# Attention rounds in another order: the last values' low half ahead of choosing experts, positions and places later, one-hots and slot matmuls in the next round

## The reference, cut to what matters

```
x = layernorm(x + attention(x))                 # 16 heads, biases on q, k, v, out
x = layernorm(x + cross(ctx, ctx, x, mask))     # 1 head of 64
probs = softmax(x @ gate.T); topw, topi = top_k(probs, 8); topw /= topw.sum(-1)
oh = one_hot(topi); pos = (cumsum(oh) * oh).sum(-1) - 1     # a token's slot in its expert
x = layernorm(x + sum over the 8 of topw * expert(x))       # slots 512 and up are dropped
```

## Time and profile before

| what | us |
|---|---|
| median of 3 runs | 2437.91 |
| the three runs | 2436.63, 2457.16, 2437.91 |
| span of the profiled execution | 2440.0 |
| attention rounds in it | to about 1440 |

### The profile page before, as it was taken

One profiled execution on the slowest core, in us unless ns is written; L12 is line 12 of the kernel. 1 busy time (PEld: TensorE's weight loads), 2 busy tenths in 40 slices (PEclk: granted clock), 3 DMA queues, 4 the chain that ended last, 5 costly groups with the idle time before them and its releaser, 6 DMA issues.

```text
span 2440.0 us, 43737 instructions
## 1 busy us (share of the span) xinstructions
PE 2110.9 (87%) x15590; PEld 1281.1 (53%) x15590; DVE 1495.3 (61%) x2527; ACT 1198.8 (49%) x2878; POOL 1150.7 (47%) x865
## 2 busy tenths in 40 slices
PE   7898998998899899889989669888888888888891
PEld 5565666666566666656666334444444444444440
DVE  5567678768767876876787764444444444444443
ACT  6675565666556655655655313333333333333334
POOL 2454455455445544544554314444444544454542
PEclk9999999999999999999999779999999999999995
DMA  5211110110111011001101127665555656665648
GB/s 187 79 40 32 36 41 22 47 34 27 33 34 39 21 47 34 31 29 34 39 21 39 53 61 216 149 146 146 146 146 146 147 146 147 151 152 145 152 70 292
DMA packets 110249, 217.13 MB, mean 89 GB/s; under 512 B 10224, under 2 KB 32752, under 8 KB 110192
## 3 DMA queue, kind: packets, MB, share of 16 engines
q1 hardware_dynamic: 81248, 148.20, 17.7%
q0 software_dynamic: 28944, 68.17, 15.2%
HBM read 156.58 MB, written 59.77 MB: 89 GB/s over the span
## 4 chain that ended last, share of the span: by engine, by line
PE 43%; issue 15%; DMA 14%; POOL 12%; DVE 10%; ACT 5%; POOLq 1%; DVEq 0%; SPq 0%; ACTq 0%
PE bank L476 23%; DMA arena_p<-x_rows,cur_from 8%; PE bank L812 7%; DMA acc_rows<-arena_wo,cur_to 6%; POOL arena_p L1706 3%; PE bank L542 3%; PE bank L554 3%; POOL arena_p L1615 3%; POOL acc_rows L1712 3%; PE bank L799 2%; DVE s_max L1147 2%; DVE x L1194 2%; ACT arena_p L887 1%; PE bank L514 1%; POOL qk L1610 1%
## 5 line engine op out<-in xcount | busy, mean ns | idle before, releaser
L476 PE MATMUL bank<-arena_v,arena_wo 128*128 128x512 f16 x2304 | 502.7, 379 | 1.1 <-issue 1.1
L1615 POOL TENSOR_TENSOR arena_p<-arena_p,s_rden 128x1024 f32<-128x1024 f32 x128 | 272.6, 2130 | 430.7 <-DVE s_rden L1155 430.7
L1712 POOL DMA_INDIRECT acc_rows<-arena_wo,cur_to x128 | 202.3, 1581 | 446.4 <-ACT arena_wo L1086 400.2
L476 PE MATMUL bank<-xt,arena_wo 128*128 128x256 f16 x3072 | 379.9, 283 | 4.2 <-DVE arena_wo L1116 4.0
L476 PEld LDWEIGHTS bank<-arena_v,arena_wo 128*128 128x128 f16 x2304 | 225.4, 98 | 272.9 <-issue 1.6
L476 PEld LDWEIGHTS bank<-xt,arena_wo 128*128 128x128 f16 x3072 | 301.6, 102 | 75.6 <-issue 29.2
L887 ACT ACTIVATE arena_p<-bank,s_neg 128x256 f32<-128x256 f32 x512 | 235.5, 474 | 170.6 <-DVE s_neg L1150 170.6
L1116 DVE SCALAR_TENSOR_TENSOR arena_v<-bank,arena_v 128x512 f16<-128x512 f32 x192 | 130.4, 688 | 281.8 <-ACT arena_v L1064 213.7
L1116 DVE SCALAR_TENSOR_TENSOR arena_wo<-stage,arena_wo 128x3072 f16<-128x3072 f32 (+2 forms) x74 | 182.0, 2461 | 184.0 <-ACT arena_wo L959 163.2
L812 PE MATMUL bank<-arena_wo 128*128 128x512 f16 x1152 | 294.0, 410 | 0.7 <-DVE arena_wo L1552 0.7
L1706 POOL DMA_INDIRECT arena_p<-x_rows,cur_from x128 | 228.0, 1782 | 56.0 <-issue 29.3
(11 more groups left out here) (170 smaller groups left out, 3318.4 us busy)
## 6 DMA issues: line engine op xcount, KB each, us to landing
stage<-wguT SPq DMA_DIRECT2D x32, 1536.0 KB, 8.1
stage<-wdnT SPq DMA_DIRECT2D x32, 768.0 KB, 9.5
xt<-xT SPq DMA_DIRECT2D x16, 512.0 KB, 5.1
xr<-x_rows SPq DMA_DIRECT2D x16, 512.0 KB, 3.9
stage<-ctxT SPq DMA_DIRECT2D x16, 512.0 KB, 3.7
x_rows<-x SPq DMA_DIRECT2D x16, 512.0 KB, 2.9
acc_rows<-x SPq DMA_DIRECT2D x16, 512.0 KB, 4.1
arena_wo<-acc_rows SPq DMA_DIRECT2D x8, 1024.0 KB, 10.8
```

What stands on the lines that cost most here:

```text
L476: mm = pe.matmul(out_ap, lhs(a, i), rhs(c, i), start=(n == 0 and i == 0), stop=(n == 2 and i == chunks - 1))
L1615: gp.tensor_tensor(rows, rows, s_rden[:, j % 2, :].unsqueeze(2).to_broadcast([P, 4, S]), ALU.mult)\
L1712: gp.indirect_dma_start(acc_rows, bass.IndirectOffsetOnAxis(ap=cur_to[:, k, c:c + 1], axis=0), y[:, k, c, :], None, compute_op=ALU.add).th ...
```

## The change

Parts of each round stand at other places; no computation is added or left out.
- DVE: `values_lo(b, 3)` comes ahead of `choose`; `choose` stands between the two `x1_lo` of step 6 and loses its last five operations to a new function `share`. `places` goes from step 6 to step 7. `share` and `tell` go to the start of the next round, behind `masked`. The one-hots of the first half go from step 7 and behind it to steps 0 and 1 of the next round, those of the second half from steps 0 and 1 to steps 3 and 4 of that round, with their `add_slots` behind them.
- PE: `positions` goes to step 7, `fill_slots(f, 0)` from step 0 to step 2, `fill_slots(f, 1)` from step 2 to step 4. In step 1 `cross_turn` and `cross_weigh` go behind q and k of pair 1, with `values(b, 1)` between them.
- ACT: `exp2` goes behind the exponentials of pair 6; `turned2_hi` goes to the end of step 1, ahead of `values_hi(b, 1)`, and `o2_high` behind that.
- POOL: `normalise2` goes behind the scaling of pair 6.
- The counts of the semaphore `rt` follow the new order. `cross_q` now waits until `places` has read the positions (`POS_READ`), in place of `turn_x1(t, 1)`; `positions` waits for both `x1_lo`.
- The last three rounds (16 to 18) get the same, apart from the exceptions for `last` and `late_fill`.

```diff
@@ values (PE)
-                if g == 0 and fill:
-                    pe.wait_ge(slot_done, count(b - 3, 2, 1))
-                elif g == 0 and tail:
+                if g == 0 and tail:
                     past(pe, kv_lo, count(b - 1, 2))
                 if g:
                     pe.wait_ge(v_lo, count(b, 4, g))
-                if g == 2 and fill:
-                    pe.wait_ge(slot_done, count(b - 3, 2, 2))
+                if g >= 2 and fill:
+                    pe.wait_ge(slot_done, count(b - 3, 2, g - 1))
@@ turn_x1, cross_q, positions (PE)
                 elif t and route:
-                    pe.wait_ge(rt, count(b - 1, RT, 20))
+                    pe.wait_ge(rt_exp, count(b - 1, 1, 1))
...
-            def cross_q(b, last=False):
+            def cross_q(b, route):
                 pe.wait_ge(x1t_lo, count(b, TT, TT))
-                if last:
-                    pe.wait_ge(rt, count(b - 1, RT, 20))
+                if route:
+                    pe.wait_ge(rt, count(b - 1, RT, POS_READ))
...
                 pe.wait_ge(rt, count(b, RT, 11))
+                if tail:
+                    pe.wait_ge(x1t_lo, count(b + 1, TT, TT))
@@ work (PE)
-                step(0, [(fill and not late_fill, lambda: fill_slots(f, 0, head))])
+                step(0)
                 if head:
                     values(b, 0, tail, fill)
-                step(1, [(route, lambda: cross_turn(u))])
+                step(1)
+                if route:
+                    cross_turn(u)
+                if head:
+                    values(b, 1, tail, fill)
                 if route:
                     cross_weigh(u)
-                if head:
-                    values(b, 1, tail, fill)
-                step(2, [(late_fill, lambda: fill_slots(f, 0, head)), (route, lambda: cross_project(u, 0)),
-                         (fill and not last and not late_fill, lambda: fill_slots(f, 1, head))])
+                step(2, [(route, lambda: cross_project(u, 0)), (fill, lambda: fill_slots(f, 0, head))])
...
-                step(4, [(tail, lambda: project(t, 0, route))])
+                step(4, [(tail, lambda: project(t, 0, route)), (fill and not late_fill, lambda: fill_slots(f, 1, head))])
...
-                step(6, [(tail, lambda: turn_x1(t, 0, head, route, fill)), (route, lambda: positions(u))])
+                step(6, [(tail, lambda: turn_x1(t, 0, head, route, fill)), (late_fill, lambda: positions(u, tail))])
...
-                step(7, [(tail, lambda: ctx_kv(t)), (tail, lambda: cross_q(t))])
+                step(7, [(route and not late_fill, lambda: positions(u, tail)), (tail, lambda: ctx_kv(t)),
+                         (tail, lambda: cross_q(t, route))])
@@ work (ACT)
-                step(0, first=[(route, lambda: exp2(u))])
+                step(0, between=[(route, lambda: exp2(u))])
...
-                step(1, first=[(route, lambda: turned2_hi(u))])
+                step(1)
+                if route:
+                    turned2_hi(u)
+                if head:
+                    values_hi(b, 1)
                 if route:
                     o2_high(u)
-                if head:
-                    values_hi(b, 1)
@@ work (DVE)
+                if fill and not late_fill and not (isinstance(r, int) and r == B + 2):
+                    share(f)
+                    tell(f)
...
-                step(0, [(route, lambda: row_scales2(u))], soon=[(fill and not late_fill, lambda: add_slots(f, 0))])
-                if late_fill:
-                    slot_onehot(f, 0, 0)
-                elif fill and not last:
-                    slot_onehot(f, 1, 0)
+                step(0)
+                if route:
+                    row_scales2(u)
                 if head:
                     values_lo(b, 0)
+                if fill:
+                    slot_onehot(f, 0, 0)
...
-                step(1, [(route, lambda: turned2_lo(u)), (fill and not last, lambda: slot_onehot(f, 0 if late_fill else 1, 1))])
+                step(1, [(fill, lambda: slot_onehot(f, 0, 1))])
+                if route:
+                    turned2_lo(u)
+                if head:
+                    values_lo(b, 1)
                 if route:
                     o2_low(u)
-                if late_fill:
-                    slot_onehot(f, 1, 0)
-                if head:
-                    values_lo(b, 1)
...
-                if fill and not last:
-                    add_slots(f, 0 if late_fill else 1)
+                if fill:
+                    add_slots(f, 0)
...
+                if fill:
+                    slot_onehot(f, 1, 0)
                 if route:
                     x2_lo(u, 0)
...
                 if head and route:
                     x2_lo(u, 1)
+                if fill:
+                    slot_onehot(f, 1, 1)
...
+                if fill and not late_fill:
+                    add_slots(f, 1)
                 step(5, [(route, lambda: gate_max(u))])
                 if tail:
                     norm1(t)
-                if route:
+                if late_fill:
                     choose(u)
-                if late_fill:
                     add_slots(f, 1)
                 if head:
                     values_lo(b, 3)
...
-                step(6, [(route, lambda: places(u))])
+                step(6, [(late_fill, lambda: places(u))])
...
                 if tail:
                     x1_lo(t, 0)
-                if route:
-                    tell(u)
+                if route and not late_fill:
+                    choose(u)
                 if tail:
                     x1_lo(t, 1)
-                step(7, [(route and not late_fill, lambda: slot_onehot(u, 0, 0))])
+                step(7, [(route and not late_fill, lambda: places(u))])
                 if tail:
                     kv2_lo(t)
                     q2_low(t)
-                if route and not late_fill:
-                    slot_onehot(u, 0, 1)
@@ work (POOL)
-                if route:
-                    normalise2(u)
-                step(0)
+                step(0, [(route, lambda: normalise2(u))])
```

```diff
@@ choose and share (DVE)
+            def share(b):
+                by_row = lambda ap: ap.unsqueeze(2).to_broadcast([P, TT, NX])
                 vec.tensor_reduce(w_sum[:, :], top_p[:, :, :], AX.X, ALU.add).then_inc(rt, 1)
-                step(b, 12)
+                step(b, 17)
                 vec.reciprocal(w_rsum[:, :], w_sum[:, :]).then_inc(rt, 1)
...
                 vec.tensor_tensor(w_lo[:, :, :], w32[:, :, :], w_hi[:, :, :], ALU.subtract).then_inc(rt, 1)
```

More of the change, by code:

```diff
@@ L1650, in work, with step @@
                 pair = pairs(r, head, tail)
-                def step(s):
+                def step(s, between=()):
                     pair(normalise, s - 2)
+                    for on, run in between:
+                        if on:
+                            run()
                     if s != 4:
```

32 lines of the change are left out of this document (18 added, 14 removed).

## The result

The change makes the kernel slower: 2466.8 us (median of 6 runs, 2462.69 to 2483.27) against 2438.6 (6 runs, 2434.63 to 2457.16), ratio 1.0123 with a 95% interval of 1.0086 to 1.016. The forecast was 2463 us. The profiled span is 2460.9 us, 20.9 more than before, where the forecast had 2465.

The account below looks back on a forecast made before the run. PE with its waits was taken to set each round; 19.2 + 26.4 + 39.0 us plus 2.6 for the clock made 87.2 against 85.4, +24 us over 13 rounds, -3 and +4 outside: 2463 us median, range 2425 to 2490.

Parts of the forecast that it names:

- (i): Scores of pair 4 to the end of those of pair 6: 23.2 us becomes 19.2, a gain of 4.0.
- maxima of pair 4 (to 2.85): Step in DVE's queue after the last values' low half, claimed done 2.85 us from the start of pair 4's scores.
- lower bound of 2.5: Smallest gain allowed for (i), 2.5 us, if choosing and `places` each met a POOL operation again.
- (ii): End of pair 6's scores to `weigh` of pair 6: 24.5 us becomes 26.4, a loss of 1.9.
- under 2.5 us there makes the prediction wrong on the fast side: Sign at `cross_weigh`: about 4 us of PE wait expected; one under 2.5 us would mean the forecast time is too slow.
- (iii): From `weigh` of pair 6 to the scores of pair 4: 37.2 us becomes 39.0, a loss of 1.85.
- The clock, +2.6 us behind `cross_weigh`: Low clock behind the new 4.05 us wait at `cross_weigh` adds 2.6 us a round, between 0 and 2.8.
- three shorter waits close to another: Clock loss over shorter PE waits could add 0 to 1.4 us; counted as nothing.
- Rounds outside, +4 -3 us: Round 2 gains 3 us for the whole run; rounds 16 and 17 together lose 4 us.
- The one-hots find their gaps: Rival: chain of (ii) 2 us shorter, `cross_weigh` waits 2 us, rounds 82.6 us, 2403 us in all; chance 0.13.
- More collisions: Rival: each of four one-hots meets POOL and the clock falls twice a round, 2488 us; chance 0.12.
- the first case: As forecast: new wait at `cross_weigh` with a clock loss, 2463 us, on the 1% bound itself; chance 0.45.

Follow-up runs that it names:

- Run 4: Changed kernel with POOL's add_bias2 moved behind the scaling of pair 5 in step 7: 2442.5 us, ratio 0.9999 to the kernel before.
- run 1: Changed kernel with shares and telling put back behind the low half of q2 at the end of their own round: 2444.29 us, ratio 1.0003.
- run 2: Changed kernel with the first one-hot ahead of the low half of the first values: 2443.64 us, ratio 1.0014.
- run 12: Changed kernel with unread transposes ahead of the scores of pair 7 (14) and of `cross_weigh` (8): 2489.12 us, ratio 1.0193.
- number 7: number 6 with the second one-hot behind the low half of pair 6 as well: 2435.85 us, ratio 0.9977.
- number 6: Changed kernel with the edits of run 1, run 2 and Run 4 together: 2439.6 us, ratio 0.9989.
- run 5: Kernel before the change with only the last values' low half put ahead of choosing: 2452.52 us, ratio 1.0033.
- run 3: Changed kernel with turned2_hi ahead of the exponentials of pair 7 and turned2_lo ahead of the second one-hot: 2489.39 us, ratio 1.0199.
- run 8: number 7 with turned2_hi ahead of the exponentials of pair 7 and turned2_lo ahead of the second one-hot: 2444.16 us, ratio 1.0007.
- run 9: number 7 with 16 unread transposes of the identity ahead of `cross_weigh`: 2428.39 us, ratio 0.9945.

## Why the prediction was right, and where it was not

The time (2466.8 for 2463) and the round (87.2 for 87.2) were right; two terms in them were wrong and cancelled. That they cancelled to a few tenths of a us is luck.

- **(i), gain 4.0 us: too large.** Measured 21.75 us (818.48 to 840.23) and 21.23 in the round after, for 19.2. The step that failed is "maxima of pair 4 (to 2.85)": they ended 1.8 us later, since POOL's bias addition held the negation (821.50, 1.60 us). From there the turn of pair 4 was late, positions waited 1.88 us for 1.3, choosing took 3.5 us (826.26 to 829.74) for 2, and in every second round the clock fell over the context's keys and values. The gain was 1.5 us in the means (22.98 to 21.49), below even the lower bound of 2.5, which had been priced by just such meetings, but for choosing and `places`; the one that came was at another operation. Run 4 shows it: without the meeting (i) takes 19.8 us, 0.6 more than walked, and the time is 25 us less.
- **(ii), loss 1.9 us: right.** 26.6 us for 26.4. The scaling took 1.89 us, exponentials of pair 6 to maxima of pair 7 were 9.0 us (847.23 to 856.23), as walked. The wait at `cross_weigh` was 2.46 us for 4.05 in this round and 1.18 in the next: PE arrived later, because waits and the low clock had held it before. Chain the same, waits distributed otherwise. Runs 1 and 2 shorten the way to `cross_weigh` by 2.9 and 1.5 us, and run 12 changes the clock without changing it: the chain sets the stretch. By the forecast's own sign, "under 2.5 us there makes the prediction wrong on the fast side", the measured time should have been the lower one (2.46 and 1.18 us); the sign was wrong, since a shorter wait there came from waits ahead of it and not from a shorter chain. Against the 12 rounds the loss is 1.5 us, since (ii) before was 24.5 and 25.8 us in turn and the forecast's round had the shorter one.
- **(iii), loss 1.85 us: right.** 866.86 to 905.78 is 38.9 us for 39.0, the wait for x2 0.85 for 0.9, the slot matmuls 0.95 (887.75). It is the largest of the three terms as measured (+1.73 us), and it is read from rows alone: no run takes the one-hot or the slot matmuls out of this stretch.
- **The clock, +2.6 us behind `cross_weigh`: wrong place.** It fell in the middle of stretch (ii), over the two waits of 2.06 and 1.30 us, where it costs nothing (run 12). The forecast had named "three shorter waits close to another" and put them at nothing. Its price was too high even where it applies: with the low clock behind `cross_weigh` the way to `weigh` is 1.6 us longer in most rounds of runs 1 and 7, and 2.5 us in run 12, of which 1.5 are left in the round.
- So a round is 21.5 + 26.6 + 38.9 = 87.0, where the forecast had 19.2 + 26.4 + 39.0 + 2.6 = 87.2: 2.3 us too little in (i), 2.6 too much for the clock.
- **Rounds outside, +4 -3 us.** Measured -1.6 up to round 2 and -1.5 from round 16 to the end (+1.9 up to `cross_weigh` of round 17, -3.4 behind it). Small; the tail was walked too pessimistically.
- **The rivals.** "The one-hots find their gaps" asked for a chain 2 us shorter. Runs 1 and 2 make it 2.9 and 1.5 us shorter and gain 23 us over the change, but end level with the kernel before and not 36 us under it: with shorter chains other waits and the low clock appear. "More collisions" happened in part, at an operation of 0.17 us more than at the one-hots. A slip in the chances: half of the first case and the last two are 0.395 and not 0.42, and the other half and the second 0.475 and not 0.44.
- **The port.** The Trainium skill, SBUF — State Buffer, section "SBUF: two separate sides", calls the pair of ports that VectorE and GpSimd share an exclusive lock: of a GpSimd operation and a VectorE operation that needs the pair (two inputs in SBUF, or a two-port mode), whichever starts first has it for its whole length. The traces agree: 0.17 us became 1.60 and 0.19 became 2.23, each ending with the POOL operation beside it (823.1 and 906.2). The traces don't show in which mode these two ran. Run 4 moves the first meeting; in runs 6 and 7 the second takes its place. Why the gains of 1, 2 and 4 add so little isn't shown beyond that.

## What to carry to other kernels

A long wait on the busiest engine is not yet a loss: ask which queue delivers late, and walk that queue in order with the wait gone; if it is as long as before, the wait comes back in pieces (run 5). Cut the rounds into the same stretches before and after and compare these, since edits that act in different stretches can end at the same time of a round. When operations move, lay the moved engine's and its port neighbour's operations side by side, small ones too: an operation of 0.2 us that starts inside one of 2.4 us costs up to 2. Price a low clock only in stretches that PE sets, and as a range: here the same wait was followed by either level.

## What the runs showed of the hardware that was not expected

- The length of a wait did not settle whether the granted clock fell. Two waits of 2.06 and 1.30 us with 0.8 us of matmuls between them had it at the level of 0.50 behind them in the kernel after, while in run 3 two of 2.08 and 1.30 us passed at full clock in every second round. Of the single ones of 2.84 and 2.83 us in the earlier trace rows the first passed, and the same 3.11 us wait (run 12) dropped it in every second round and left it in the others. At `cross_weigh` 2.46 us passed in the kernel after and 2.55 us did not in number 7. A low clock stood behind each wait of 4.03 to 4.11 us that is shown.
- Rounds of different orders came out at nearly equal lengths. Means of 12 rounds are 85.33 us in the kernel before, 85.58, 85.51, 85.10, 85.33 and 85.36 in runs 2, 4, 6, 7 and 8, then 87.05 in the kernel after, and 88.75 in both run 3 and run 12, whose edits have nothing in common. An edit's time alone does not tell what it is worth in its own stretch: in run 1 a gain of 2.9 us there left 1.2 of the round. In number 6 one round of 13 lasted 82.67: in it the clock stayed up behind `cross_weigh` (3.66 us to `weigh` for 5.29), and DVE's split was waited for 0.94 us where it is about 2. What ties the lengths isn't settled; run 9 (84.34) shows that they can leave it.
- 29 or 30 more matmuls in a loop body brought the instruction queue from 36 to 135 packets and two waits of 1.7 to 2.6 us in each pass but the first. 16 or 22 more did not. Whether number or place decides is open.
